# RGCN layers on one core: weight loads move from SyncE to ScalarE's queue, and the last product's square roots and scaling move one tile back

## The reference

```python
def _rgcn_conv(x, src, dst, etype, W, root, b):
    seg = dst * num_rel + etype
    sums = jax.ops.segment_sum(x[src], seg, num_segments=num_nodes * num_rel)
    cnt = jax.ops.segment_sum(ones, seg, num_segments=num_nodes * num_rel)
    mean = (sums / jnp.maximum(cnt, 1.0)[:, None]).reshape(num_nodes, num_rel, -1)
    return jnp.einsum('nri,rio->no', mean, W) + x @ root + b

h = jax.nn.relu(_rgcn_conv(x, src, dst, etype, W1, root1, b1))
out = _layernorm(x + _rgcn_conv(h, src, dst, etype, W2, root2, b2))   # over the last axis, eps 1e-5
```

## Time and profile before

| | |
|---|---|
| median of 3 runs | 1454.06 us |
| lowest, highest | 1453.46, 1455.05 us |
| the profiled execution | 1466.17 us |
| its span, first to last instruction | 1464.3 us |
| mean granted TensorE clock | 0.994 of full speed |
| busy TensorE (PE) | 1437.1 us, 98% |
| busy VectorE (DVE) | 927.6 us, 63% |
| busy ScalarE (ACT) | 573.1 us, 39% |
| busy GpSimd (POOL) | 559.0 us, 38% |
| moved by DMA | 248.58 MB |

### The profile page before, as it was taken

How to read it: one execution, slowest core, us unless ns; L and a number is a source line. 1 busy time by engine, 2 the same in 40 slices (tenths; PEclk the granted TensorE clock), 3 DMA queues, 4 the chain that set the end, 5 groups by cost and what they waited for, 6 DMA issues and landing times.

```text
span 1464.3 us, 23621 instructions
## 1 busy us (share of the span) xinstructions
PE 1437.1 (98%) x8715; PEld 1419.6 (97%) x8715; DVE 927.6 (63%) x1475; ACT 573.1 (39%) x805; POOL 559.0 (38%) x437
## 2 busy tenths in 40 slices
PE   8999999999999899999999999999999999999997
PEld 8999999999999899999999999999999999999996
DVE  7899999857777577456771154545454454444677
ACT  4222334335444444344552233333343333433454
POOL 0000000066777686425535232434242424243552
PEclk9999999999999999999999999999999999999998
DMA  6414321358877776664463465646464656656454
GB/s 195 152 60 127 96 72 47 106 183 267 254 211 227 227 229 191 212 200 149 136 189 103 148 211 168 210 144 218 142 211 156 199 177 184 194 171 213 119 169 123
DMA packets 112523, 248.58 MB, mean 170 GB/s; under 512 B 19617, under 2 KB 87768, under 8 KB 112446
## 3 DMA queue, kind: packets, MB, share of 16 engines
q0 software_dynamic: 30880, 134.67, 31.1%
q1 hardware_dynamic: 81566, 112.88, 24.1%
HBM read 192.77 MB, written 65.49 MB: 176 GB/s over the span
## 4 chain that ended last, share of the span: by engine, by line
PE 89%; DVE 6%; issue 3%; ACT 1%; DMA 1%; SPq 0%; ACTq 0%; POOLq 0%
PE prod L767 70%; PE agg L809 14%; DVE g_low L1029 2%; PE agg L904 2%; PE agg L767 2%; PE prod L809 1%; PE agg L758 1%; DVE g_high L1029 1%; ACT g_high L628 1%; DVE acc L1046 1%; DVE g_low L1033 1%; DMA x_rows<-in_x 0%; PE agg L907 0%; DVE stats L1401 0%; DMA raw<-y,bucket_index 0%
## 5 line engine op out<-in xcount | busy, mean ns | idle before, releaser
L767 PE MATMUL prod<-w_high,h_high 128*128 128x384 f32 x2064 | 693.5, 336 | 0.0
L767 PE MATMUL prod<-w_high,h_low 128*128 128x384 f32 x2064 | 690.4, 335 | 0.0
L767 PE MATMUL prod<-w_low,h_high 128*128 128x384 f32 x2064 | 690.1, 334 | 0.0
L519 POOL DMA_INDIRECT raw<-y,bucket_index x310 | 410.5, 1324 | 538.5 <-DVE g_low L1033 220.1
L653 ACT ACTIVATE y_stage<-prod 128x384 f32<-128x384 f32 x320 | 157.7, 493 | 781.6 <-PE prod L767 631.1
L1033 DVE TENSOR_TENSOR g_low<-raw,g_high 128x768 fp32r<-128x768 f32 x240 | 220.4, 956 | 370.6 <-ACT g_high L631 312.4
L767 PEld LDWEIGHTS prod<-w_high,h_high 128*128 128x128 f32 x2064 | 388.1, 188 | 0.1
L767 PEld LDWEIGHTS prod<-w_low,h_high 128*128 128x128 f32 x2064 | 388.0, 188 | 0.0
L767 PEld LDWEIGHTS prod<-w_high,h_low 128*128 128x128 f32 x2064 | 387.8, 188 | 0.0
L631 ACT ACTIVATE g_high<-raw 128x768 fp32r<-128x768 f32 x240 | 189.9, 839 | 1.9 <-DMA raw<-y,bucket_index 1.5
L809 PE MATMUL agg<-g_high,one_hot 128*128 128x384 f32 x616 | 159.8, 340 | 10.1 <-DVE g_low L1033 7.6
(11 more groups left out here) (179 smaller groups left out, 992.7 us busy)
## 6 DMA issues: line engine op xcount, KB each, us to landing
y<-y_stage SPq DMA_DIRECT2D x320, 168.0 KB
w_raw<-in_w_all SPq DMA_DIRECT2D x35, 1152.0 KB
y<-y_stage SPq DMA_DIRECT2D x320, 19.5 KB
raw<-y,bucket_index POOLq DMA_INDIRECT x310
acc<-in_x POOLq DMA_DIRECT2D x10, 375.0 KB, 6.4
x_rows<-in_x SPq DMA_DIRECT2D x10, 336.0 KB
out<-acc SPq DMA_DIRECT2D x10, 336.0 KB
w_raw<-in_w_all SPq DMA_DIRECT2D x2, 576.0 KB, 4.6
```

What stands on the lines that cost most here:

```text
L519: pool.indirect_dma_start(raw_rows(slot), None, y[0:written * N, :], bass.IndirectOffsetOnAxis(ap=bucket_index[:, at_column:at_column + 1] ...
L767: mm = pe.matmul(to, left[:, k, t * P:(t + 1) * P], right[:, h, k, :], start=(k == 0 and left is h_high and right is w_high), stop=(n == 0 ...
```

## The change

The loads of weights leave SyncE's program and enter ScalarE's, from the units of product 2 on (the third product; what q = 0 asks for stays with SyncE). A load now stands after a given step's copy (`load_at`), with the same two waits. ScalarE's high parts of the weights move to later steps in q = 4 to 7 (`high_at`), and VectorE's low parts of q = 4 to 6 one step back in two of four places. In `finish(1)` the root, the factor and shift, and the scaling are done for tile t - 1 where they were done for tile t, the root between the first and the second block's high part; in `finish(0)` the two loads are written into the loop and behind it. ScalarE's loop over the second layer's relations is one turn shorter and its last turn is written out. The core of the diff:

```diff
@@ sync
             def load_unit(q, h):
                 u = unit(q, h)
-                if not (isinstance(q, int) and u == 0):
-                    sp.wait_ge(w_high_ready, u)
-                    sp.wait_ge(w_low_ready, u)
...
-                sp.dma_start(w_raw[:], w).then_inc(w_loaded, 16)
+                sp.wait_ge(w_high_ready, u)
+                sp.wait_ge(w_low_ready, u)
+                sp.dma_start(w_raw[:], weights_of(q, h)).then_inc(w_loaded, 16)
...
-                    if s == 8:
-                        load_unit(q + 1, 0)
-                    if s == 14:
-                        load_unit(q + 1, 1)
...
-            load_unit(ROOT1 + 1, 0)
-            load_unit(ROOT1 + 1, 1)
@@ scalar
+            def load_unit(q, h):
+
+                u = unit(q, h)
+                act.wait_ge(w_high_ready, u)
+                act.wait_ge(w_low_ready, u)
+                act.dma_start(w_raw[:], weights_of(q, h)).then_inc(w_loaded, 16)
...
-            def matrix(q, yc, actions=lambda s: [], after=None):
+            def matrix(q, yc, actions=lambda s: [], after=None, high_at=(1, 11), load_at=(8, 15)):
...
-                    if s == 1:
+                    if s == high_at[0]:
                         high_of_unit(q, 1)
-                    if s == 11:
+                    if s == high_at[1]:
                         high_of_unit(q + 1, 0)
+                    if s in load_at:
+                        load_unit(q + 1, load_at.index(s))
...
-            matrix(0, 0, turning_x)
-            matrix(1, 1)
+            matrix(0, 0, turning_x, load_at=())
+            matrix(1, 1, load_at=(9, 17))
...
                 for t in range(T):
+                    if layer == 0 and t == 2:
+                        load_unit(q + 1, 0)
                     if layer == 0 and t == T - 2:
                         high_of_unit(q + 1, 0, STEPS * q + FIRST_HALF)
-                    if t + 1 < T:
-                        bucket(g, t + 1)
+                    rows = list(enumerate(tile_range(g, t + 1))) if t + 1 < T else []
+                    for b, i in rows[:1]:
+                        high_of_tile(g, i, tiles(g) * (t + 1) + b)
+                    if layer and t:
+                        deviation(t - 1)
+                    for b, i in rows[1:]:
+                        high_of_tile(g, i, tiles(g) * (t + 1) + b)
...
-                    else:
-                        deviation(t)
-                        if t + 1 < T:
-                            norm(t)
...
+                    if layer and t:
+                        norm(t - 1)
+                if layer:
+                    deviation(T - 1)
+                else:
+                    load_unit(q + 1, 1)
...
-            matrix(2, 2, after=copied_ahead(2))
-            matrix(3, 3, after=copied_ahead(3))
+            matrix(2, 2, after=copied_ahead(2), load_at=(8, 16))
+            matrix(3, 3, after=copied_ahead(3), load_at=(10, 17))
             for q in range(TABLE_END, ROOT1 - 1):
-                matrix(q, q, pair_of(q))
-            matrix(ROOT1 - 1, ROOT1 - 1, one_relation(R - 2, None))
+                matrix(q, q, pair_of(q), high_at=(3, 12), load_at=(9, 17))
+            matrix(ROOT1 - 1, ROOT1 - 1, one_relation(R - 2, None), high_at=(2, 11))
@@ vector, finish
                     if (layer, t) == (1, T - 1):
+                        scale_of(t - 1)
                         last_moments(g, t)
                         continue
                     add(g, R - 1, t)
+                    if layer and t:
+                        scale_of(t - 1)
...
-                    if layer and t + 1 < T:
-                        scale_of(t)
-                    elif layer == 0 and t:
+                    if layer == 0 and t:
...
-            in_parts = ((4, 0, K // 2), (7, K // 2, K), (13, 0, K // 2), (16, K // 2, K))
+            in_parts = ((5, 0, K // 2), (7, K // 2, K), (14, 0, K // 2), (16, K // 2, K))
```

More of the change, by code:

```diff
@@ L385, in bank_of, with weights_of @@
             return s % BANKS
+        def weights_of(q, h):
+            of = ([R] + [r - 1 + (r > R // 2) for r in range(1, R)] + [R // 2, Q - 1] +
+                  list(range(R + 2, 2 * R + 1)) + [R + 1])
+            m = of[q] if isinstance(q, int) else q
+            return w_all[bass.ds(m, 1), :, h * HALF:(h + 1) * HALF].rearrange("o (k p) n -> p (o k) n", p=P)
         block = ctx.enter_context(nc.Block())
@@ L718, in finish @@
                 for t in range(T):
+                    if layer == 0 and t == 2:
+                        load_unit(q + 1, 0)
                     if layer == 0 and t == T - 2:
                         high_of_unit(q + 1, 0, STEPS * q + FIRST_HALF)
-                    if t + 1 < T:
-                        bucket(g, t + 1)
+                    rows = list(enumerate(tile_range(g, t + 1))) if t + 1 < T else []
[5 more added lines that the diff above has]
+                        high_of_tile(g, i, tiles(g) * (t + 1) + b)
                     if layer == 0:
                         relu(t)
-                        if t:
-                            high_of_turn(1, t - 1)
-                    else:
-                        deviation(t)
-                        if t + 1 < T:
-                            norm(t)
+                    if layer == 0 and t:
+                        high_of_turn(1, t - 1)
+                    if layer and t:
[4 more added lines that the diff above has]
+                    load_unit(q + 1, 1)
             def deviation(t):
@@ L739, in norm @@
                                scale=std[:, t % 2, 1:2]).then_inc(normed, 1)
-            matrix(2, 2, after=copied_ahead(2))
-            matrix(3, 3, after=copied_ahead(3))
+            matrix(2, 2, after=copied_ahead(2), load_at=(8, 16))
+            matrix(3, 3, after=copied_ahead(3), load_at=(10, 17))
             for q in range(TABLE_END, ROOT1 - 1):
-                matrix(q, q, pair_of(q))
-            matrix(ROOT1 - 1, ROOT1 - 1, one_relation(R - 2, None))
+                matrix(q, q, pair_of(q), high_at=(3, 12), load_at=(9, 17))
+            matrix(ROOT1 - 1, ROOT1 - 1, one_relation(R - 2, None), high_at=(2, 11))
             finish(0)
             matrix(ROOT1 + 1, stored_before(1, 0), last_turns)
-            with act.Fori(1, R) as r:
+            with act.Fori(1, R - 1) as r:
                 matrix(r + ROOT1 + 1, stored_before(1, r), one_relation(r + R - 1, None))
+            matrix(ROOT2 - 1, stored_before(1, R - 1), one_relation(2 * R - 2, None))
             finish(1)
```

## The result

| | before | changed |
|---|---|---|
| median of 4 runs | 1454.03 us | 1445.72 us |
| lowest, highest | 1453.46, 1455.05 us | 1444.84, 1446.08 us |
| the profiled execution | 1466.17 us | 1445.62 us |
| its span | 1464.3 us | 1443.2 us |

The change takes 8.3 us off: the ratio is 0.9941, with a 95% interval of 0.9924 to 0.9958. Faster was forecast, at 1443.7 with a range of 1437 to 1450. The two profiles are 21.1 us apart, 12.8 more than the timed runs: the profiled execution of the kernel before was a long one (1466.17 us, where its timed runs end at 1455.05), and that of the changed kernel is an ordinary one. So no difference between the two traces may be taken for a gain unless a timed run bears it out.

What follows compares the result with a forecast made beforehand. TensorE, busy 98% of the span, was taken to bound the kernel, except in the last product, where a chain over ScalarE and VectorE did. From the median: 1454.06 - 6.7 - 1.7 - 2.0 = 1443.7 us, range 1437 to 1450.

Steps and rivals of the forecast that it cites:

- (1): Last product: root and scaling one tile back free TensorE's pace and bring the end forward; -6.7 us, other end -2.8.
- VectorE's own idle time before the first low part: Sign in the last product: this wait on ScalarE, 1.93 us in each tile, would be gone.
- the ring: Last product: gapless chain of ScalarE and VectorE work from root to root, 9.08 us a tile against TensorE's 8.68.
- the tail: End of the last product: the addition of bucket 8 starts at 1444.5 and not at 1451.64, 7.1 us earlier.
- the pace: Last product: TensorE sets the time per tile, 0.40 us less a tile for seven tiles, 2.8 us.
- (2): q = 4, step 2: with the weights' high parts at step 3, rows are cut 2.1 us earlier; -1.7 us.
- (3): q = 5: stores no longer stand behind SyncE's load waits, sparing TensorE's stall and half clock; -2.0 us, bounded by 0 and 6.6.
- The rival in which the stores are held by bytes: Stores are held by bytes and not by the queue, so the loads' stall stays: 1445.7 us, chance 0.15.
- (4): TensorE's remaining idle places, behind copies late with no stated releaser: 0 us, with 4.4 gain as the other end.
- (5): q = 1 and 3: loads asked for two steps and one step ahead; staging banks hide any lateness; nothing.
- The slower rival: q = 4 to 6: unit asked for at step 9 is late for step 12 and holds the rows; 1468 us, chance 0.05.

Runs made afterwards that it cites:

- the first set: Runs on one chip: last product alone, loads alone, changed kernel without the loads, and the kernel before profiled again; kernel before at median 1453.46 us.
- the second profile of before: The kernel before, unchanged, profiled once more: 1453.62 us, span 1451.7.
- the third chip: Chip of the last runs: high parts alone, changed kernel again, and two further edits with loads on either queue; kernel before at median 1462.26 us.
- the version with the loads on SyncE's queue: Changed kernel with q = 7 high parts at step 1, tile 8's factor and shift after the first half's statistics, all weight loads on SyncE: 1454.02 us.

## Why the prediction was right, and where it was not

**(1) Root and scaling one tile back: -6.7 forecast, -7.1 measured** alone, and 7.1 between the two traces of that set. Each step of the working is in the trace: roots 8.67 apart, the addition on the bucket's end, TensorE held up nowhere between start-up and the last bucket. VectorE's own idle time before the first low part did not go away (1.52 us instead of 1.93): it now waits for a block that ScalarE, by the program, cuts when TensorE frees a slot, and not for the ring. I wrote that it would go, and that was a wrong sign to look for. I counted the tail and the pace as two pieces that add, and in the two traces they do: from the start-up stall to bucket 8 it is 2.5 us less (1427.41 - 1366.71 against 1444.05 - 1380.83), and from bucket 8 to the last scaling 4.4 less (1439.42 - 1427.41 against 1460.48 - 1444.05). What I missed is that the second piece depends on how early the ring is cut: cut for the last three tiles alone, only 2.1 of the 4.4 came.

**(2) High parts later: -1.7 forecast, -1.0 in the medians** of the first set, inside the noise. The 1.29 + 0.39 went. What failed is that I worked the term out for q = 4 to 6 and took q = 7 along in silence: there the move from step 1 to step 2 puts the weights' 2.12 us ahead of the rows of step 3, and brings 1.29 back. By the traces that leaves 0.4; no trace accounts for the rest of the 1.0, which may be noise. Its larger worth I missed altogether: it makes the loads on ScalarE's queue harmless. With the high part at step 11 the unit is two steps old, and the same loads cost 6.9 us; at step 12 it is three.

**(3) Loads off SyncE's queue: -2.0 forecast, nothing measured**, three times: 1445.40 without against 1445.72 with (two sets), 1452.46 without against 1452.53 with, 1454.02 without against 1453.74 with. The second pair is the sharpest: its interval ends 1.6 us below no change, short of the 2.0. The mechanism on SyncE was right (13 us at its waits in all three traces of the first set with the loads on SyncE, stores with it), and so was the late copy, up to 4.3 us. The failed step is the last one, from the late copy to TensorE: I carried the 3.81 us over at a third, and it is 0.94 in the second profile of before, and nothing in the first set's two traces with the new last product and the loads still on SyncE's queue. Even on the third chip, in the version with the loads on SyncE's queue, the copy of step 19 came 5.40 us late and TensorE did not stand for it: it lists no idle time between 482.52 and its next stall at 513.94, which follows copies held by `remote`. The rival in which the stores are held by bytes named 1445.7, the very time measured, but its reason is not what happened: after the change the stores do go out step by step. The Trainium skill (DMA: Bandwidth & Descriptors, "Issuing engines are not separate DMA queues") would have given this term nothing, and it was right on the time, though not because nothing changed: the sequencer's hold did go away, beside work that had slack for it.

**(4) Other idle places: 0 forecast.** They were not removed by the change; the second profile of the kernel before has none of them: the stall of 498 with its half clock (6.6) and these places (4.4) are 11.0 of the 12.8 us by which the profiles differ beyond the runs. The third chip's traces have stalls of this kind, with the loads on either queue. Which signal is late there is open: the profile names `remote`, that is, a releaser that it has no record of.

**(5) Early loads: nothing**, and nothing was seen; 1.9 us of ScalarE's waiting in all.

**The slower rival** had a chance of 0.05 and a price of 5.3 us late for a load of 18.8. In q = 5 of the changed kernel a load takes 11.7 us and is wanted after 13.8 (439.17 to 453.01): a margin of 2 us, less than half a step. The price per late microsecond was right (one for one); that of a fall of the clock was 1.9 to 2.7 and not 2.8. The chance was fair for this change and would have been far too low for its neighbour with the high part at step 11.

The forecast of 1443.7 missed the median of 1445.72 by 2.0 us: the term of the loads that wasn't there. The errors of (1) and (2) nearly cancel, which is luck; the mechanism of (1), which carries 7 of the 8 us, was right.

## What to carry to other kernels

Before a stall seen in one profile is put into a sum, ask whether the median has room for it: here an execution 12 us over the median held stalls that a second profile hadn't. Where a late piece meets the bounding engine through buffers (a copy through four PSUM banks) it may be 4 us late for nothing, and where it stands in one queue ahead of that engine's next input (a unit's high part ahead of the rows) each microsecond goes through in full. And a change of several parts should be read as pairs too: the part that brought 1 us at most by itself was what kept another from costing 7.

## What the runs showed of the hardware

The kernel before ran 9 to 10 us longer on one chip than on two others (before: 1462.26 against 1453.46 and 1452.46), and the changed kernel's gain was 4.0 us there instead of 8.3. I had taken the distance of a profile from its median for chance within one chip; these runs say that a chip can be like that in nearly every run. The granted clock fell to half after a wait of TensorE of 5 to 7 us in q = 4 to 6, three times of three, and did not in q = 5 behind one of 2.26. That is no bound: in the profile of the high parts alone, on the slower chip, the bucket behind a wait of 1.59 ran at the lower clock (TensorE had stood 0.39 and 0.38 us in the 4 us before it):

```profile
469.56 0.98 PE L809 MATMUL agg<-g_high,one_hot 128*128 128x384 f32 x2 [1.59 <-DVE g_low L1033]
```
